# A state-space and butterfly block on one core: projection onto delta, B, C in two column halves, state products in two row halves of the array

## The chip, the cores and the metric

One Trainium2 chip, one of its cores. The metric is the device time of one execution in microseconds, the median over several. Engines: TensorE (PE), VectorE (DVE), ScalarE (ACT), GpSimd (POOL), SyncE (SP). All data is float32; three-part products in float32r are used in some places.

## The reference, cut to what matters

Input `x` is (2, 2048, 256). A state-space block and a feed-forward block are added to it one after the other, each on a layer norm.

```python
xz = einsum('bld,ed->ble', layernorm(x), in_proj_w); x_inner, z = split(xz, 2)
x_conv = silu(causal_conv4(x_inner) + conv_b)            # 512 channels
x_dbl = einsum('bld,ed->ble', x_conv, x_proj_w)          # 33 columns
delta = softplus(x_dbl[..., 0]); B = x_dbl[..., 1:17]; C = x_dbl[..., 17:]
# for every token: h = h * exp(delta * A) + x_conv * (delta * B);  y = sum_n h * C
y = (y + x_conv * D) * silu(z)
x = x + einsum('bld,od->blo', y, out_proj_w)
# feed-forward: expand to 1024, butterfly, gelu, butterfly, contract to 256
x = x + ffn(layernorm(x))
```

## The kernel before, in words

The sequence is cut into four tiles of 512 tokens; a loop runs over them, and each tile holds both batch rows (b0 and b1). The butterfly stages are multiplied into the weights in a preparation at the start, which runs beside tile 1. Every engine has its own instruction stream with an order written out by hand (`first_half`, `second_half`), and engines meet in semaphores. PE writes into three rings of PSUM banks: `wide` (3 banks, in-projection, x-projection, y, out-projection, up), `small` (3 banks) and `acc` (2 banks, down). `WIDE_ORDER` lists the uses of the wide ring in the order of PE (L60 to L66); use number n has bank n modulo 3 (L104), and `free` makes PE wait until all earlier takes of that bank are done.

In a tile, for one batch row: the in-projection (L727) gives x_inner and z; ACT copies and applies the first tap (L1060), DVE the three others (L1346), ACT the silu (L1069). `x_projection` (L731 to L737) multiplies the four channel blocks of xc with w_x, 33 columns, into rows 0 to 32 of one bank. ACT copies the result to xdT (L1077). `tokens_first` (L745) transposes xc in 16 pieces into four small banks, which ACT and DVE copy to x_tok (two each), and `xd_tokens_first` (L753) transposes xdT in four pieces; DVE copies 33 columns of each as xd (L1374) and goes on to softplus (L1377 to L1402), which yields delta, dB and the rest of the scan's inputs.

The scan is computed in matrices: m_mat (L1481, L1486) holds how tokens of a group of 128 act on each other, and `state` holds the state that enters each of the four groups, at rows 32c to 32c+15 for group c; c_startT has rows 32c to 32c+15 filled for the 128 tokens of group c alone. `state_inputs` (L795) makes four products of 16 weight columns each, at rows 32c of a bank. `advance_state` (L1454) makes the states. `ssm_output` (L820 to L837) then computes y: for channel blocks in pairs (0, 1), (2, 3), four products of x_tok with m_mat for each block (L829), then one product of state with c_startT over all 128 rows and 512 tokens for each block (L836). `gate` (L1488 to L1496) reads one y bank per block with xc and skip, and multiplies with z. After four gates the out-projection starts (L847), which waits for all of them.

The order on PE: b0's `x_projection`, `tokens_first`, `xd_tokens_first`, four in-projections of b1, the scan's small products mixed with three more in-projections, `x_projection` of b1, `ssm_output` of b0, `tokens_first` and `xd_tokens_first` of b1, out-projection of b0, small products of b1, in-projection 7 of b1, transposes for the feed-forward. Then the feed-forward of b0 (L858 up, L869 down), with `ssm_output` of b1 between up block 3 (with down block 1) and up block 4, and the out-projection of b1 after down block 2; then the feed-forward of b1. On DVE b0's gates are followed by the copies of x_tok and xd of b1, softplus of b1, the first residual (L1502) and the second normalisation (L1255).

## Time and profile before

| what | value |
|---|---|
| median of 3 runs | 631.44 us (630.95 to 631.99) |
| the profiled execution | 632.72 us, its span 630.8 us |
| PE busy | 560.5 us, 89% of the span |
| DVE busy | 443.5 us, 70% |
| ACT busy | 303.1 us, 48% |
| POOL busy | 123.9 us, 20% |
| mean granted clock of TensorE | 0.951 |
| DMA | 12.88 MB, mean 20 GB/s |

The span is that of the instructions of the program in the one execution that was profiled. Busy time is the union of an engine's instructions. A float32 product of PE leaves two records in the trace. The ends of PE's records are modelled, so consecutive records overlap a little; the distance between starts is the more exact figure. The granted clock is 1.00 at 2.4 GHz and 0.50 at 1.2 GHz.

### The profile page before, as it was taken

The page shows a single profiled execution, that of the slowest core. Times are in us where ns is not written, and L with a number is a line of the kernel's source. Part 1 is how long each engine was busy: PE and PEld are TensorE (multiplying, and loading weights), DVE is VectorE, ACT ScalarE, POOL GpSimd, SP SyncE. Part 2 cuts the span into 40 slices and gives each one's busy share as a digit, 9 for nine tenths or more (in the row PEclk, how much of TensorE's full clock was granted, in tenths as well). Part 3 has the DMA queues.
Part 4 walks back from the last instruction along what each step waited for, and adds up shares of the span by engine and source line. Part 5 has one row for each costly group of instructions (what it writes and reads, how often), then busy time and mean ns, then how long its engine had stood idle before and what let it go on. Part 6 is the DMA issues. An engine that isn't in the chain of part 4 may idle for free.

```text
span 630.8 us, 8980 instructions
## 1 busy us (share of the span) xinstructions
PE 560.5 (89%) x2996; PEld 436.9 (69%) x2996; DVE 443.5 (70%) x883; ACT 303.1 (48%) x511; POOL 123.9 (20%) x104
## 2 busy tenths in 40 slices
PE   4989776679999997979999989979999988979996
PEld 3747345647899773747899665847899664848895
DVE  5748868876556789877556699887555699977432
ACT  3655739146055766044144866054254865162252
POOL 4213100240012032250021042250020041340010
PEclk9988876899999999979999998979999999979999
DMA  8332020010010100010000000000100000000000
GB/s 239 4 22 4 0 66 2 1 35 2 3 64 2 34 1 2 0 34 0 33 33 0 33 0 0 0 33 0 33 33 0 33 0 0 0 0 2 0 34 34
DMA packets 33067, 12.88 MB, mean 20 GB/s; under 512 B 22003, under 2 KB 32499, under 8 KB 33044
## 3 DMA queue, kind: packets, MB, share of 16 engines
q1 hardware_dynamic: 31444, 9.96, 7.3%
q10 hardware_dynamic: 1600, 2.62, 1.2%
q8 instruction: 13, 0.21, 0.2%
q14 instruction: 10, 0.08, 0.0%
HBM read 8.39 MB, written 4.19 MB: 20 GB/s over the span
## 4 chain that ended last, share of the span: by engine, by line
PE 58%; DVE 23%; ACT 8%; issue 7%; DMA 2%; POOL 1%; DVEq 0%; ACTq 0%; POOLq 0%
PE acc L869 14%; PE wide L858 12%; PE wide L727 8%; DVE xc L1346 6%; PE wide L847 4%; PE wide L829 4%; PE wide L836 4%; PE wide L736 3%; DVE x1b_xn L1255 2%; PE small L717 2%; DVE soft L1385 2%; PE acc L656 1%; PE small L806 1%; DVE diag_sum L1475 1%; PE small L784 1%
## 5 line engine op out<-in xcount | busy, mean ns | idle before, releaser
L1031 ACT ACTIVATE hid_f<-wide,bias_up 128x512 f32<-128x512 f32 x64 | 44.0, 687 | 139.3 <-PE acc L869 127.4
L1346 DVE SCALAR_TENSOR_TENSOR xc<-xi,taps,xc 128x512 f32<-128x512 f32 x96 | 91.0, 958 | 6.5 <-ACT xc L1060 4.2
L1363 DVE TENSOR_TENSOR hid_low<-hid_f,hid_high 128x512 fp32r<-128x512 f32 x64 | 44.3, 692 | 68.8 <-ACT hid_high L1132 68.2
L869 PE MATMUL acc<-w_down_high,hid_high 128*128 128x256 f32 x256 | 73.9, 289 | 1.5 <-DVE hid_low L1363 1.5
L869 PE MATMUL acc<-w_down_low,hid_high 128*128 128x256 f32 x256 | 71.8, 281 | 0.0
L869 PE MATMUL acc<-w_down_high,hid_low 128*128 128x256 f32 x256 | 71.7, 280 | 0.0
L847 PE MATMUL wide<-w_out,yg 128*128 128x256 f32 x256 | 56.9, 380 | 0.0
L537 POOL TENSOR_TENSOR c_place<-xd,row_in_block 128x1024 f32<-128x1024 f32 x8 | 15.5, 1938 | 208.8 <-DVE xd L1374 208.8
L727 PE MATMUL wide<-xnT_high,w_in_high 128*128 128x512 f32 x128 | 54.9, 429 | 0.0
L858 PE MATMUL wide<-xnT_high,w_up_high 128*128 128x512 f32 x128 | 53.4, 417 | 0.0
L869 PEld LDWEIGHTS acc<-w_down_high,hid_high 128*128 128x128 f32 x256 | 48.2, 188 | 6.6 <-DVE hid_low L1363 4.5
L847 PEld LDWEIGHTS wide<-w_out,yg 128*128 128x128 f32 x256 | 48.0, 190 | 6.6
L727 PE MATMUL wide<-xnT_low,w_in_high 128*128 128x512 f32 x128 | 52.2, 408 | 0.0
L727 PE MATMUL wide<-xnT_high,w_in_low 128*128 128x512 f32 x128 | 52.0, 406 | 0.0
L858 PE MATMUL wide<-xnT_high,w_up_low 128*128 128x512 f32 x128 | 50.3, 393 | 0.0
L858 PE MATMUL wide<-xnT_low,w_up_high 128*128 128x512 f32 x128 | 50.1, 391 | 0.0
L869 PEld LDWEIGHTS acc<-w_down_low,hid_high 128*128 128x128 f32 x256 | 48.3, 189 | 1.8
L501 POOL TENSOR_TENSOR rstd<-var_eps,minus_half 128x4 f32<-128x4 f32 x16 | 19.0, 1186 | 154.5 <-DVE var_eps L1250 154.2
L869 PEld LDWEIGHTS acc<-w_down_high,hid_low 128*128 128x128 f32 x256 | 48.4, 189 | 0.0
L829 PEld LDWEIGHTS wide<-m_mat,x_tok 128*128 128x128 f32 x256 | 33.6, 209 | 18.2 <-ACT xdT L1031 10.3
L829 PE MATMUL wide<-m_mat,x_tok 128*128 128x128 f32 x256 | 35.1, 296 | 10.0 <-ACT xdT L1031 9.1
L1132 ACT ACTIVATE hid_high<-hid_f 128x512 fp32r<-128x512 f32 x64 | 40.6, 634 | 2.0
(184 smaller groups left out, 1136.4 us busy)
## 6 DMA issues: line engine op xcount, KB each, us to landing
x_in<-in_L_attn_x_dram SPq DMA_DIRECT2D x8, 512.0 KB, 3.6
out_dram<-x1b_xn SPq DMA_DIRECT2D x8, 512.0 KB, 2.9
xc<-in_L_attn_in_proj_w_dram ACTq DMA_DIRECT2D x2, 512.0 KB, 6.6
xc<-in_L_ffn_W_exp_dram ACTq DMA_DIRECT2D x1, 1024.0 KB, 9.3
low_w<-in_L_ffn_W_con_dram SPq DMA_DIRECT2D x1, 1024.0 KB, 5.6
raw_out<-n_L_attn_out_proj_w_dram ACTq DMA_DIRECT2D x1, 512.0 KB, 10.3
low_w<-in_L_ffn_up_weights_dram SPq DMA_DIRECT2D x14, 4.0 KB
low_w<-_L_ffn_down_weights_dram SPq DMA_DIRECT2D x14, 4.0 KB
```

The source lines that it names most:

```text
L501: pool.tensor_tensor(rstd[:, slot, :], var_eps[:, slot, :], minus_half[:, :], ALU.pow)\
L727: last = pe.matmul(bank[:, :], w_in[w][:, m, e * P:(e + 1) * P], xnT[x][:, m, :], start=n == 0, stop=n == MB * len(PASSES) - 1)
L736: last = pe.matmul(bank[0:XD, :], w_x[:, g, :], xc[b][:, g, :], start=g == 0, stop=g == CB - 1)
L829: pe.matmul(bank[:, c * P:(c + 1) * P], x_tok[:, c, g * P:(g + 1) * P], m_mat[:, c * P:(c + 1) * P], start=c == 0, stop=False, skip_group_ ...
L836: mark_written(pe.matmul(tile_of("y", g, b)[:, :], state[b][:, g * P:(g + 1) * P], c_startT[:, :], start=False, stop=True, skip_group_chec ...
L847: last = pe.matmul(bank[:, q * DM:(q + 1) * DM], yg[:, g, c * P:(c + 1) * P], w_out[:, g, :], start=g == 0, stop=g == CB - 1)
L858: last = pe.matmul(bank[:, :], w_up[w][:, m, j * P:(j + 1) * P], xnT[x][:, m, :], start=n == 0, stop=n == MB * len(PASSES) - 1)
L869: last = pe.matmul(acc[:, c, :], hid[h][:, j % HRING, c * P:(c + 1) * P], w_down[w][:, j, 0:DM], start=j == 0 and c % 2 == 0 and n == 0, s ...
L1031: ins = act.activation(out_ap, in_ap, how.pop("func"), **how)
L1132: act.activation(hid[0][:, j % HRING, :], hid_f32[:, j % HRING, :], ACT.Copy).then_inc(hid_high.handle, 1)
L1346: ins = dve.scalar_tensor_tensor(xc[b][:, e, :], xi[:, e, tap:tap + TILE], taps[:, e, tap:tap + 1], xc[b][:, e, :], ALU.mult, ALU.add)
L1363: dve.tensor_tensor(hid[1][:, j % HRING, :], hid_f32[:, j % HRING, :], hid[0][:, j % HRING, :].bitcast(F32), ALU.subtract).then_inc(hid_re ...
```

## The change

`x_projection`: w_x becomes 64 columns wide for each channel block (33 filled, the rest zero), blocks 0 and 2 write rows 0 to 63 of the bank, blocks 1 and 3 rows 64 to 127. ACT copies all 128 rows to xdT. Instead of four transposes of xdT with the identity there are four products of xdT with `fold`, a 128x33 matrix that adds rows j and 64+j. `ssm_output`: a y bank holds 256 tokens of two channel blocks instead of 512 tokens of one. The product of the states is cut into rows 0 to 63 (token half 0) and rows 64 to 127 (token half 1), each 256 columns wide and each writing its own bank; PE waits for both banks of a pair before the pair's first product. `gate` reads its block from the two neighbouring banks with one pattern, waits for both at the first block of a pair, and releases both after the first operation of the second block. The wide ring gets its banks from a list, so that the banks of a pair are neighbours. In the preparation w_x is cleared by POOL in place of xdT, `fold` is made by DVE ahead of its other constants and waited for by PE at preparation step 4, and bias_raw lies in yg.

```diff
-    + [("y", g, 0) for g in range(CB)] + [("out", 0, 0), ("out", 1, 0), ("in", 7, 1)]
-    + [("up", j, 0) for j in range(4)] + [("y", g, 1) for g in range(CB)]
+    + [("y", n, 0) for n in range(CB)] + [("out", 0, 0), ("out", 1, 0), ("in", 7, 1)]
+    + [("up", j, 0) for j in range(4)] + [("y", n, 1) for n in range(CB)]
...
+WIDE_BANKS = [2, 0, 1] * 5 + [2, 0] + [1, 2, 0, 1] + [2, 0, 1] + [2, 0, 1, 2] + [0, 1, 1, 2] + [0, 1, 2] * 4 + [0, 1]
...
-        w_x = sb("w_x", [P, CB, XD])
+        w_x = sb("w_x", [P, CB, HALF])
+        fold = sb("fold", [P, XD])
...
-        wide = [ctx.enter_context(nc.psum_tensor(f"wide{i}", [P, TILE], F32)) for i in range(RING)]
+        wide_banks = ctx.enter_context(nc.psum_tensor("wide", [P, RING, TILE], F32))
+        wide = [wide_banks[:, i, :] for i in range(RING)]
...
-        bias_raw = sb("bias_raw", [P, 2, DM])
+        bias_raw = yg[:, 0, :].rearrange("p (n d) -> p n d", d=DM)
...
-            pool.memset(xdT[:, :], 0.0).then_inc(zeroed, 1)
+            pool.memset(w_x[:, :, :], 0.0).then_inc(zeroed, 1)
...
                     wait_taken(pe, ("w_x", 0, 0))
+                    pe.wait_ge(folded, 1)
...
-                    last = pe.matmul(bank[0:XD, :], w_x[:, g, :], xc[b][:, g, :], start=g == 0, stop=g == CB - 1)
+                    at = HALF * (g % 2)
+                    last = pe.matmul(bank[at:at + HALF, :], w_x[:, g, :], xc[b][:, g, :], start=g < 2, stop=g >= CB - 2,
+                                     skip_group_check=True)
...
-                    last = pe.transpose(bank[:, c * P:(c + 1) * P], xdT[:, c * P:(c + 1) * P], ident[:, :])
+                    last = pe.matmul(bank[:, c * P:c * P + XD], xdT[:, c * P:(c + 1) * P], fold[:, :], start=True, stop=True)
...
-                for pair in ((0, 1), (2, 3)):
-                    for g in pair:
-                        bank = tile_of("y", g, b)
-                        free(pe, k, "y", g, b)
-                        if g == 0:
-                            read(pe, k, "moff", 0, b)
+                for pair in range(2):
+                    banks = [tile_of("y", 2 * pair + h, b) for h in range(2)]
+                    for h in range(2):
+                        free(pe, k, "y", 2 * pair + h, b)
+                    if pair == 0:
+                        read(pe, k, "moff", 0, b)
+                    for q in range(2):
+                        g = 2 * pair + q
                         for c in range(GR):
-                            pe.matmul(bank[:, c * P:(c + 1) * P], x_tok[:, c, g * P:(g + 1) * P],
-                                      m_mat[:, c * P:(c + 1) * P], start=c == 0, stop=False, skip_group_check=True)
-                    for g in pair:
-                        if g == 0:
-                            read(pe, k, "ct", 0, b)
-                            pe.wait_ge(first_state.handle, first_state.value(k, b, 1))
-                            pe.wait_ge(states_ready.handle, states_ready.value(k, b, 1))
-                        mark_written(pe.matmul(tile_of("y", g, b)[:, :], state[b][:, g * P:(g + 1) * P], c_startT[:, :],
-                                               start=False, stop=True, skip_group_check=True), "y", g, b)
+                            at = q * HALF_TILE + c % 2 * P
+                            pe.matmul(banks[c // 2][:, at:at + P], x_tok[:, c, g * P:(g + 1) * P],
+                                      m_mat[:, c * P:(c + 1) * P], start=q == 0 and c % 2 == 0, stop=False,
+                                      skip_group_check=True)
+                    if pair == 0:
+                        read(pe, k, "ct", 0, b)
+                        pe.wait_ge(first_state.handle, first_state.value(k, b, 1))
+                        pe.wait_ge(states_ready.handle, states_ready.value(k, b, 1))
+                    for q in range(2):
+                        g = 2 * pair + q
+                        for h in range(2):
+                            rows = slice(2 * SLOT * h, 2 * SLOT * (h + 1))
+                            last = pe.matmul(banks[h][:, q * HALF_TILE:(q + 1) * HALF_TILE],
+                                             state[b][rows, g * P:(g + 1) * P],
+                                             c_startT[rows, h * HALF_TILE:(h + 1) * HALF_TILE],
+                                             start=False, stop=q == 1, skip_group_check=True)
+                            if q == 1:
+                                mark_written(last, "y", 2 * pair + h, b)
...
-                take(k, "xp", 0, b, xdT[0:XD, :], tile_of("xp", 0, b)[0:XD, :])
+                take(k, "xp", 0, b, xdT[:, :], tile_of("xp", 0, b)[:, :])
...
+                dve.tensor_tensor(fold[:, :], ident[:, 0:XD], ident[:, HALF:HALF + XD], ALU.add).then_inc(folded, 1)
...
-                    dve.tensor_tensor(bias_out[:, :], bias_raw[:, 0, :], bias_raw[:, 1, :], ALU.add)
+                    link_setup(dve.tensor_tensor(bias_out[:, :], bias_raw[:, 0, :], bias_raw[:, 1, :], ALU.add))
...
-                written(dve, k, "y", g, b)
-                mark_read(dve.scalar_tensor_tensor(yg[:, g, :], xc[b][:, g, :], skip[:, g:g + 1],
-                                                   tile_of("y", g, b)[:, :], ALU.mult, ALU.add), "y", g, b)
-                read(dve, k, "y", g, b)
+                pair, q = divmod(g, 2)
+                bank = WIDE.bank(("y", 2 * pair, b))
+                both = wide_banks[:, bank:bank + 2, q * HALF_TILE:(q + 1) * HALF_TILE]
+                if q == 0:
+                    for h in range(2):
+                        written(dve, k, "y", 2 * pair + h, b)
+                halves = "p (h t) -> p h t"
+                ins = dve.scalar_tensor_tensor(yg[:, g, :].rearrange(halves, h=2),
+                                               xc[b][:, g, :].rearrange(halves, h=2), skip[:, g:g + 1],
+                                               both, ALU.mult, ALU.add)
+                if q == 0:
+                    link(ins)
+                else:
+                    mark_read(ins, "y", 2 * pair, b)
+                    read(dve, k, "y", 2 * pair, b)
+                    dve.sem_inc(WIDE.read[WIDE.bank(("y", 2 * pair + 1, b))], 1)
```

## Rows read from the trace of the kernel before

**Rows 1.** The page, part 4: the chain that ended last, shares by line.
```profile
PE acc L869 14%; PE wide L858 12%; PE wide L727 8%; DVE xc L1346 6%; PE wide L847 4%; PE wide L829 4%; PE wide L836 4%; PE wide L736 3%; DVE x1b_xn L1255 2%; PE small L717 2%; DVE soft L1385 2%; PE acc L656 1%; PE small L806 1%; DVE diag_sum L1475 1%; PE small L784 1%
```
**Rows 2.** Windows: length, busy us of PE, PEld, DVE, ACT, POOL, granted clock, DMA.
```profile
541.00:557.00 16.00, 11.79 (x64) 9.88 (x62) 15.10 (x42) 1.75 (x5) 10.31 (x7) 0.94 0.00 0
...
561.00:626.00 65.00, 64.26 (x388) 54.59 (x380) 31.31 (x52) 27.48 (x40) 5.32 (x3) 0.99 0.03 9
```
**Rows 3.** Timeline, PE, b0 of tile 4: start us, us, what, [idle before].
```profile
498.94 3.62 PE L736 MATMUL wide<-xc,w_x 128*33 128x512 f32 x8
...
504.39 0.65 PE L753 MATMUL small<-ident,xdT 128*128 128x128 f32 x4
```
**Rows 4.** Timeline, PE, around the output of b0, tile 4.
```profile
524.87 1.15 PE L816 MATMUL small<-c_hat,b_hat 128*128 128x128 f32 x8 [1.47 <-DVE diag L1470]
525.95 1.05 PE L795 MATMUL small<-x_tok,b_end 128*16 128x512 f32 x8
...
530.98 2.05 PE L829 MATMUL wide<-m_mat,x_tok 128*128 128x128 f32 x16 [0.43 <-DVE m_mat L1486]
533.40 1.96 PE L836 MATMUL wide<-c_startT,state 128*128 128x512 f32 x4 [0.37 <-DVE state L1454]
535.19 1.95 PE L829 MATMUL wide<-m_mat,x_tok 128*128 128x128 f32 x16
536.97 1.88 PE L836 MATMUL wide<-c_startT,state 128*128 128x512 f32 x4
```
**Rows 5.** Timeline, ACT, b0 of tile 4.
```profile
500.34 1.08 ACT L1031 ACTIVATE xnT_high<-small 128x512 fp32r<-128x512 f32 x2
502.66 0.59 ACT L1031 ACTIVATE xdT<-wide 33x512 f32<-33x512 f32 x1 [1.24 <-PE wide L736]
```
**Rows 6.** Timeline, DVE, b0 of tile 4.
```profile
505.27 0.28 DVE L1374 COPY xd<-small 128x132 f32<-128x132 f32 x1
...
534.63 0.75 DVE L1493 SCALAR_TENSOR_TENSOR yg<-xc,skip,wide 128x512 f32<-128x512 f32 x1 [0.59 <-PE wide L836]
...
536.02 0.74 DVE L1493 SCALAR_TENSOR_TENSOR yg<-xc,skip,wide 128x512 f32<-128x512 f32 x1
...
538.04 0.75 DVE L1493 SCALAR_TENSOR_TENSOR yg<-xc,skip,wide 128x512 f32<-128x512 f32 x1 [0.55 <-PE wide L836]
```
**Rows 7.** Timeline, PE, x-projection of b1 in tile 3.
```profile
388.69 3.59 PE L736 MATMUL wide<-xc,w_x 128*33 128x512 f32 x8 [1.35 <-ACT xc L1069]
392.22 2.05 PE L829 MATMUL wide<-m_mat,x_tok 128*128 128x128 f32 x16
```
**Rows 8.** Timeline, PE, preparation and tile 1.
```profile
74.09 5.11 PE L736 MATMUL wide<-xc,w_x 128*33 128x512 f32 x8 [2.51 <-ACT xc L1069]
...
100.52 3.78 PE L829 MATMUL wide<-m_mat,x_tok 128*128 128x128 f32 x16 [9.15 <-ACT xdT L1031]
```
**Rows 9.** Timeline, PE, the output of b1 in tile 4.
```profile
577.09 1.95 PE L829 MATMUL wide<-m_mat,x_tok 128*128 128x128 f32 x16
578.88 1.88 PE L836 MATMUL wide<-c_startT,state 128*128 128x512 f32 x4
...
583.41 0.81 PE L847 MATMUL wide<-w_out,yg 128*128 128x256 f32 x3
```
**Rows 10.** Timeline, DVE, the gates of b1 in tile 4.
```profile
577.92 0.74 DVE L1493 SCALAR_TENSOR_TENSOR yg<-xc,skip,wide 128x512 f32<-128x512 f32 x1
...
579.94 0.75 DVE L1493 SCALAR_TENSOR_TENSOR yg<-xc,skip,wide 128x512 f32<-128x512 f32 x1 [0.55 <-PE wide L836]
...
582.10 0.69 DVE L1496 TENSOR_TENSOR yg<-yg,z 128x512 f32<-128x512 f32 x1
```
**Rows 11.** Lines by form: xcount | busy us, mean ns | idle before.
```profile
L1529 DVE TENSOR_TENSOR x1b_xn<-acc,x1b_xn 128x1024 f32<-128x1024 f32 x8 | 9.8, 1225 | 6.3 <-PE acc L869 6.3
```
**Rows 12.** Windows with a stop of PE in tiles 4 and 3.
```profile
516.00:522.00 6.00, 2.99 (x14) 1.81 (x14) 5.93 (x8) 2.42 (x4) 4.23 (x3) 1.00 0.00 0
375.00:384.00 9.00, 6.00 (x16) 3.39 (x15) 8.89 (x11) 2.83 (x5) 5.19 (x3) 0.64 0.00 0
```

More of the change, by code:

```diff
@@ L53 @@
 SLOT = 32
+HALF_TILE = TILE // 2
+HALF = P // 2
 LOW = 7
@@ L78 @@
 HRING = 2
-FIRST_HALF_STEPS, VECTOR_STEPS = 45, 54
+FIRST_HALF_STEPS, VECTOR_STEPS = 47, 58
 class Signal:
@@ L94, with __init__ @@
 class Banks:
-    def __init__(self, nc, ctx, name, tiles, order):
+    def __init__(self, nc, ctx, name, tiles, order, banks=None):
         self.tiles, self.order = tiles, order
+        banks = banks or [n % len(tiles) for n in range(len(order))]
+        assert len(banks) == len(order)
         self.written = [ctx.enter_context(nc.semaphore(f"{name}{i}_written")) for i in range(len(tiles))]
@@ L102, in __init__ @@
         self.place, self.products, self.takes = {}, [0] * len(tiles), [0] * len(tiles)
-        for n, use in enumerate(order):
-            bank = n % len(tiles)
+        for use, bank in zip(order, banks):
             before = self.takes[bank]
@@ L217, in bass_preln_ssm_butterfly_ffn @@
         rstd = sb("rstd", [P, 2 * BATCH, GR])
-        wide = [ctx.enter_context(nc.psum_tensor(f"wide{i}", [P, TILE], F32)) for i in range(RING)]
+        wide_banks = ctx.enter_context(nc.psum_tensor("wide", [P, RING, TILE], F32))
+        wide = [wide_banks[:, i, :] for i in range(RING)]
         small = [ctx.enter_context(nc.psum_tensor(f"small{i}", [P, TILE], F32)) for i in range(RING)]
         acc = ctx.enter_context(nc.psum_tensor("acc", [P, GR, DM], F32))
-        WIDE = Banks(nc, ctx, "wide", wide, WIDE_ORDER)
+        WIDE = Banks(nc, ctx, "wide", wide, WIDE_ORDER, WIDE_BANKS)
         SMALL = Banks(nc, ctx, "small", small, SMALL_ORDER)
@@ L318, in bass_preln_ssm_butterfly_ffn @@
         rates_exp = sem("rates_exp")
+        folded = sem("folded")
         made = sem("made")
@@ L636, in make @@
                     for g in range(CB):
-                        last = pe.transpose(bank[:, g * XD:(g + 1) * XD], raw_x[:, g * P:(g + 1) * P], ident[0:XD, 0:XD])
+                        last = pe.transpose(bank[:, g * HALF:g * HALF + XD], raw_x[:, g * P:(g + 1) * P], ident[0:XD, 0:XD])
                 elif name == "w_out":
@@ L996, in receive @@
                 if name == "w_x":
-                    ins = act.activation(w_x[:, :, :].rearrange(flat), bank[:, 0:CB * XD], ACT.Copy)
+                    act.wait_ge(zeroed, 1)
+                    ins = act.activation(w_x[:, :, 0:XD], bank[:, 0:CB * HALF].rearrange("p (g w) -> p g w", w=HALF)[:, :, 0:XD],
+                                         ACT.Copy)
                 elif name == "w_out":
```

## The prediction

> **What bounds the kernel now.** I read the page's chain that ended last first: most of it lies on PE's lines, with L1346 of the vector engine among them, and the lines of the change hold 4% (L829), 4% (L836) and 3% (L736) of it [rows 1]. Then the timeline of one steady tile (the last, 484 to 626 us) by engine, since a share says nothing of which engine ends a stage. It shows stages with different limits. From the x-projection of batch 0 to the end of its second normalisation the vector engine sets the pace: between 541 and 557 us it is busy for 15.10 of 16.00 us and PE for 11.79 [rows 2]. From 561 us to the end PE is busy for 64.26 of 65.00 us [rows 2]: a microsecond won or lost on PE there is one of the whole. Between them lie hand-overs, which the other rows show. Four tiles run, each with a call of every function for batch 0 (b0) and batch 1 (b1); tile 1 overlaps the preparation of the weights and goes otherwise.
>
> **X-projection.** Now eight records (an fp32 product leaves two) of 512 columns in 3.62 us, in one column group [rows 3]. With neighbouring g in two column halves, two run at once. No row has two halves, but the state-input products (L795) write four column groups of 512 columns with the same operand size, and their eight records take 1.05 us, not 3.6 [rows 4]: one column group's own time. So two halves should take half, some 1.85 us: 1.75 us less per call (the end of the last record doesn't shrink); bounds are 0 (no overlap) and 1.8. Behind it the four transposes of xdT (0.65 us [rows 3]) become four fp32 products, eight records that each load 128 weight columns; the nearest row, eight fp32 records of 128 columns (L816), takes 1.15 us, the last of them 1.1 after the first began [rows 4]. I take +0.45 us, bounds 0 and +0.5.
> What reaches the end, b0, tiles 2 to 4: the first xp copy on ACT stands at 502.66 because it waited 1.24 us for L736; before it ACT finishes xnT_high at 500.34+1.08 = 501.42 [rows 5]. So the copy can come 1.24 us earlier, not 1.75, and x_tok, whose banks the later transposes need, goes with it. The transposes then end sooner by 1.24, and the products of xdT cost 0.45 more; part of this is hidden, since the vector engine's copy of x_tok stands between. The vector engine takes xd at 505.27 [rows 6]; I put it at 504.3, **1.0 us earlier**, and all of the vector stage follows. Three times: -3.0.
> b1, tiles 2 and 4: after L736 the first L829 waits 0.43 us, until 530.98, for m_mat of the vector engine [rows 4]. The 1.75 us become idle time of PE: **0**. In tile 3 L736 started late (388.69, after a wait for ACT's xc) and L829 follows it without a gap [rows 7]; there 1.3 us count, as the last activation limits it: -1.3. In the preparation (tile 1) b0's x-projection follows the activations one by one, and nothing comes of it; b1's, 5.11 us and partly at a lower clock [rows 8], stands ahead of products on which a load and the mixing wait. About 1.5 us there, less 0.45 for the xdT products of b0: -1.0.
>
> **State products.** Two (four records) of 512 columns take 1.88 us modelled and hold PE for 1.72, since 0.16 of a group lies beside its successor [rows 9, 4]. They become four products of 64 rows by 256 columns, eight records; if both row halves run at once, 0.86 us. Nothing in this trace uses row halves. Bounds: 0.86 (the column groups' behaviour, L795) and 1.72 (all eight in turn: 2048 product columns, as now). I take 0.86, as the only packed row of the trace overlaps fully. The Trainium skill's page "TensorE: Matmul & The Clock Gate" (Part 3, measured speedup) gives 3.07x for four row tiles, not 4x; an estimate by that efficiency is 1.12 us a pair, and 3.6 us more for the kernel. Changing the array's shape: L795 starts 0.07 us before its predecessor's modelled end, where products of one shape overlap by 0.16 to 0.17 [rows 4]; so 0.1 us per change, two in the path of each call: 0.2 us. The skill's "TensorEngine Tiling (Array Packing)" (Key Properties) says that a mode change drains the engine; by this rule, the trace agrees, at 0.1 us.
>
> **The wait that this needs.** The y banks now hold token halves of two channel blocks, so gate 0 needs the whole first pair, and a bank is free only when gate 1 has read it. WIDE_BANKS gives the second pair of b0 banks 0 and 1, of which 1 is the first pair's; that of b1 banks 1 and 2, 1 again. PE asks for both banks before any product of the second pair. Now y2 needs neither, and y3 only gate 0. So PE stops after the first pair until gate 1's first operation ends, with all 16 x_tok products, the state products, and then the transposes of b1 (or up block 4 and down block 2) queued behind it; gates 2 and 3 wait for the same.
> b0, tiles 2 and 4: state products start at 533.40, gate 0 at 534.63, when y0 is done [rows 4, 6]; with 0.86 us for the whole pair that stays. Gate 1's first operation ends at 536.02+0.74 = 536.76 [rows 6]. Then 1.78 us of L829 (start to start [rows 4]) and 0.86 of L836, and the 0.37 us from the end of the stream to a gate (533.40+0.86 to 534.63): gate 2 at about 539.8, against 538.04 now [rows 6]. **+1.8**, with shape changes +2.0. Its cover would be slack behind the gates, and there is none: x_tok, xd and softplus follow at once, and the vector engine has 0.9 us idle in the next 16 [rows 2]. Tile 3 runs the same once its x-projection is shorter. Three times: +6.0. Tile 1's second pair waits 9.15 us for ACT's xdT [rows 8], long after gate 1: 0.
> b1, all tiles, PE-bound: L829 of the second pair at 577.09, its L836 at 578.88 [rows 9]. After: gate 1's first operation ends at 577.92+0.74 = 578.66 [rows 10], 0.1 to hand on, 1.78+0.86: PE is through at 581.4, against 578.88+1.72 = 580.6. Gates 2 and 3 start at 581.8 and take 2.85 us (579.94 to 582.10+0.69 = 582.79 [rows 10]) to 584.65. Up block 4 and down block 2 (2.8 us, from 580.6 to 583.41) fill PE till 584.2, so the out-projection waits for the gates: 584.75 against 583.41 [rows 9], **+1.35**, with shape changes +1.5. Four times: +6.0.
>
> **Small edits.** The gate reads two banks through one pattern: the final add, 1024 columns over two banks, takes 1225 ns [rows 11], 0.61 us per 512, so no surcharge; bounds 0 and 0.1 a gate. The copy of xdT takes 128 rows for 33, the same 512 columns as its neighbours (1.08 us for two, 0.59 for xdT [rows 5]): 0. `fold` is one add of 33 columns, less than the 0.28 us of a 132-column copy [rows 6], in the preparation ahead of the x-projection: covered by the wait for activations there, 0.2 if not. The memset of w_x takes the place of xdT's and is smaller; bias_raw within yg and its link add one wait of under 0.1.
>
> **Sum.** -3.0 -1.3 -1.0 +6.0 +6.0 = +6.7 us on the profiled execution's 632.72, which is 1.28 above the median of 631.44. Against the median: **638.0 us**.
>
> **Rivals.** (1) The row halves don't overlap: +0.86 a pair, 1.72 a call, seven calls: +12, 650 us. For it: no row shows row halves; against: L795. (2) The clock falls in the new gap. PE stops for about 2.5 us between the pairs, and in b0 already idles 2 us shortly before. Two stretches, in each of which PE stands still for 3 us, show a granted clock of 1.00 (from 516) and 0.64 (from 375), a mean over the levels 2.4 and 1.2 GHz [rows 12]: it can go either way. At half clock the second pair costs 2.6 us more; in three to four of seven calls: 646 us. (3) The other side, faster: the stop between the pairs is not there, or is filled, since the first pair is read sooner than I say. Its place is the wait for y's banks; it decides from the point where gate 1's read ends before the first pair's successor could start. Then b1 wins 1.72 a call (-6.9), b0 0.86 three times (-2.6), and the x-projection's 5.3 stand: -15, 617 us. Half of that if the stop is shorter only. Against it: gate 1 needs gate 0's two operations before it, 2.1 us after the pair. (4) Gains and stops even out: if the x-projection gives its full 1.75 in b0 and the stops cost 1 each, the sum is within 1 us of zero.
>
> **Chances.** Forecast 0.55, (1) 0.10, (2) 0.14, (3) 0.10, (4) 0.11. A measurement can tell about 0.2%, 1.3 us, from no change. Faster 0.12 (all of 3, a little of 4), same 0.08, slower 0.80. The range of the forecast alone is 634 to 642 (clock and bounds); taking in most of (2), part of (1) and the slow end of (4): 632 to 648.
>
> **What would show it.** Right: L736's eight records in about 1.9 us; L836's eight in about 1.0; PE idle some 2.5 us before every second L829 group of tiles 2 to 4, ended by the vector engine's yg; xd about 1 us earlier after the x-projection; the out-projection of b1 waiting for the gates. Wrong: no idle time before the second L829 group, L836 pairs at 1.8 us, or half clock behind the gap.

## The result, and the profile after

| | before | after |
|---|---|---|
| median | 631.20 us (630.52 to 631.99, 4 runs) | 648.68 us (644.92 to 650.34, 4 runs) |
| ratio, 95% interval | | 1.0264 (1.0237 to 1.0290) |
| profiled execution, its span | 632.72, 630.8 us | 649.47, 647.7 us |
| mean granted clock of TensorE | 0.951 | 0.941 |

Slower, as forecast, but by 17.5 us at the medians (16.9 at the spans) and not by 6.8: 0.7 us above the range. After's lines are numbered anew: L745 is the x-projection (before L736), L763 xdT by `fold` (L753), L842 x_tok by m_mat (L829), L853 the state products (L836), L868 the out-projection (L847), L1523 and L1532 the gate (L1493, L1496).

The page of after, parts 1 and 4, beside [rows 1]:
```profile
PE 555.4 (86%) x3092; PEld 446.1 (69%) x3092; DVE 443.8 (69%) x884; ACT 302.3 (47%) x511; POOL 122.7 (19%) x104
...
PE acc L890 13%; PE wide L879 9%; DVE xc L1370 7%; PE wide L735 5%; PE wide L842 5%; PE wide L868 4%; DVE yg L1523 3%; PE wide L853 3%; DVE x1b_xn L1278 2%; DVE diag_sum L1499 2%; PE small L725 2%; PE small L755 2%; DVE yg L1532 2%; PE acc L663 2%; DVE soft L1409 2%
```
PE is busy for 5 us less than before (560.5) in a span 17 us longer. The gate (L1523, L1532) is new in this list: 5% of the chain, some 30 us. Groups of instructions by line and form:
```profile
L1523 DVE SCALAR_TENSOR_TENSOR yg<-xc,skip,wide 128x512 f32<-128x512 f32 x32 | 23.8, 744 | 29.2 <-PE wide L853 29.1
L1532 DVE TENSOR_TENSOR yg<-yg,z 128x512 f32<-128x512 f32 x32 | 22.1, 692 | 3.0 <-DVE yg L1523 2.3
L853 PE MATMUL wide<-c_startT,state 64*128 64x256 f32 x128 | 19.5, 425 | 1.1 <-DVE state L1478 1.1
L745 PE MATMUL wide<-xc,w_x 128*64 128x512 f32 x64 | 19.2, 611 | 8.3 <-ACT xc L1092 8.3
```
The gate's read costs no more through two banks (744 ns; 743 before), but DVE waits 29.1 us for L853 ahead of it. The view of the one line L842 says what PE waited for ahead of it (us, times):
```profile
  ACT xdT L1054: 9.9, 1
  DVEq L1531: 9.8, 4
  DVE yg L1523: 6.8, 3
```
The first is tile 1's, as before [rows 8]. The other seven are new: a stop of 2.3 to 2.4 us before the second pair in every call but that one, released by gate 1's read (DVEq L1531 is the release of the second bank that stands behind it). Timeline, PE, the output of b0 in tiles 3 and 4 (start us, us, what, [idle before]), beside [rows 4, 7]:
```profile
399.33 2.05 PE L842 MATMUL wide<-m_mat,x_tok 128*128 128x128 f32 x16 [0.42 <-DVE m_mat L1510]
401.75 1.14 PE L853 MATMUL wide<-c_startT,state 64*128 64x256 f32 x8 [0.37 <-DVE state L1478]
405.17 2.05 PE L842 MATMUL wide<-m_mat,x_tok 128*128 128x128 f32 x16 [2.28 <-DVE yg L1523]
407.15 1.14 PE L853 MATMUL wide<-c_startT,state 64*128 64x256 f32 x8
408.21 2.00 PE L755 MATMUL small<-ident,xc 128*128 128x128 f32 x16
...
541.97 2.05 PE L842 MATMUL wide<-m_mat,x_tok 128*128 128x128 f32 x16
544.39 1.14 PE L853 MATMUL wide<-c_startT,state 64*128 64x256 f32 x8 [0.37 <-DVE state L1478]
547.80 3.49 PE L842 MATMUL wide<-m_mat,x_tok 128*128 128x128 f32 x16 [2.28 <-DVE yg L1523]
551.22 1.13 PE L853 MATMUL wide<-c_startT,state 64*128 64x256 f32 x8
555.60 1.75 PE L868 MATMUL wide<-w_out,yg 128*128 128x256 f32 x7 [0.40 <-DVE yg L1532]
```
The same instructions behind the same stop take 2.05 us in tile 3 and 3.49 in tile 4. The windows over tiles 4 and 3 (second and third line) show why; the first line is one of the preparation (length, busy us of PE, PEld, DVE, ACT, POOL, granted clock):
```profile
128.00:140.00 12.00, 8.38 (x32) 5.65 (x30) 8.17 (x17) 3.82 (x8) 6.40 (x4) 0.73 0.15 46
546.00:552.00 6.00, 4.20 (x24) 3.99 (x24) 2.40 (x4) 0.00 (x0) 0.00 (x0) 0.72 0.00 0
403.00:409.00 6.00, 3.83 (x31) 3.34 (x32) 3.37 (x5) 0.09 (x1) 0.00 (x0) 1.00 0.00 0
```
The granted clock is a mean of 1.2 and 2.4 GHz in the first two lines, and 2.4 GHz throughout in the third. Of the seven second pairs three ran for the most part at half clock (at 161, 261 and 548 us). On DVE the stop looks like this (timeline, gates of b0 in tile 4), beside [rows 6]:
```profile
545.61 0.75 DVE L1523 SCALAR_TENSOR_TENSOR yg<-xc,skip,wide 128x512 f32<-128x512 f32 x1 [0.59 <-PE wide L853]
...
547.00 0.74 DVE L1523 SCALAR_TENSOR_TENSOR yg<-xc,skip,wide 128x512 f32<-128x512 f32 x1
547.90 0.69 DVE L1532 TENSOR_TENSOR yg<-yg,z 128x512 f32<-128x512 f32 x1 [0.16 <-DVE yg L1523]
552.48 0.75 DVE L1523 SCALAR_TENSOR_TENSOR yg<-xc,skip,wide 128x512 f32<-128x512 f32 x1 [3.88 <-PE wide L853]
...
555.37 1.28 DVE L1393 COPY x_tok<-small 128x512 f32<-128x512 f32 x2
```
And b1 of tile 4 on PE at full clock, beside [rows 9]:
```profile
588.13 1.95 PE L842 MATMUL wide<-m_mat,x_tok 128*128 128x128 f32 x16
590.01 1.13 PE L853 MATMUL wide<-c_startT,state 64*128 64x256 f32 x8
593.59 2.05 PE L842 MATMUL wide<-m_mat,x_tok 128*128 128x128 f32 x16 [2.44 <-DVEq L1531]
595.57 1.13 PE L853 MATMUL wide<-c_startT,state 64*128 64x256 f32 x8
...
599.98 1.32 PE L868 MATMUL wide<-w_out,yg 128*128 128x256 f32 x5 [0.22 <-DVE yg L1532]
```

**Where the time came from.** How late each stage of after begins against the same stage of before, from the starts of L842, L868 and L745, gives the terms of the 16.9 us:

| term | forecast | measured |
|---|---|---|
| x-projection, L745 of b0 to the first L842 of b0, tiles 2, 3, 4 | -1.0, -2.3, -1.0 | -0.85, -2.9, -0.9 |
| output of b0, first L842 to L868, tiles 2, 3, 4 | +2.0 each | +3.6, +2.7, +3.6 |
| output of b1, first L842 to L868, tiles 1 to 4 | +1.5 each | +3.5, +1.9, +1.9, +2.0 |
| preparation and tile 1 up to b1's output | -1.0 | +1.65 |
| everything between | 0 | +0.7 |
| sum | +6.7 | +16.9 |

The three calls with a half-clock second pair are the +3.6, +3.6 and +3.5; without the clock a call of b0 costs +2.1 and one of b1 +1.9 to +2.0. Tile 3 needs care: there before's first pair had no wait for m_mat and state (9.46 us from L829 to L847, in tiles 2 and 4 10.06), so 0.6 us of its +2.7 is a wait that has moved, and its -2.9 holds a half clock of before (before_warm below).

### The profile page after: what moved, and what is told of

The parts are those of the page before. It is cut to its first block, busy times and chain, and to the rows that moved or that the text cites. A ratio compares the mean times of both kernels' runs of the same rounds, so it can differ in the third digit from the quotient of the medians.

```text
span 647.7 us, 9206 instructions
## 1 busy us (share of the span) xinstructions
PE 555.4 (86%) x3092; PEld 446.1 (69%) x3092; DVE 443.8 (69%) x884; ACT 302.3 (47%) x511; POOL 122.7 (19%) x104
## 4 chain that ended last, share of the span: by engine, by line
PE 47%; DVE 32%; ACT 10%; issue 8%; DMA 2%; POOL 1%; DVEq 1%; ACTq 0%; POOLq 0%
PE acc L890 13%; PE wide L879 9%; DVE xc L1370 7%; PE wide L735 5%; PE wide L842 5%; PE wide L868 4%; DVE yg L1523 3%; PE wide L853 3%; DVE x1b_xn L1278 2%; DVE diag_sum L1499 2%; PE small L725 2%; PE small L755 2%; DVE yg L1532 2%; PE acc L663 2%; DVE soft L1409 2%
## 5 line engine op out<-in xcount | busy, mean ns | idle before, releaser
L842 PE MATMUL wide<-m_mat,x_tok 128*128 128x128 f32 x256 | 40.0, 321 | 27.2 <-ACT xdT L1054 9.9
L842 PEld LDWEIGHTS wide<-m_mat,x_tok 128*128 128x128 f32 x256 | 37.1, 230 | 34.9 <-ACT xdT L1054 10.7
L868 PE MATMUL wide<-w_out,yg 128*128 128x256 f32 x256 | 57.2, 382 | 2.2 <-DVE yg L1532 1.8
L868 PEld LDWEIGHTS wide<-w_out,yg 128*128 128x128 f32 x256 | 48.0, 190 | 9.5 <-issue 2.3
L508 POOL TENSOR_TENSOR rstd<-var_eps,minus_half 128x4 f32<-128x4 f32 x16 | 17.3, 1084 | 164.2 <-DVE var_eps L1273 163.9
L1523 DVE SCALAR_TENSOR_TENSOR yg<-xc,skip,wide 128x512 f32<-128x512 f32 x32 | 23.8, 744 | 29.2 <-PE wide L853 29.1
```

Of the source, the lines that this page charges most:

```text
L508: pool.tensor_tensor(rstd[:, slot, :], var_eps[:, slot, :], minus_half[:, :], ALU.pow)\
L842: pe.matmul(banks[c // 2][:, at:at + P], x_tok[:, c, g * P:(g + 1) * P], m_mat[:, c * P:(c + 1) * P], start=q == 0 and c % 2 == 0, stop=False,
L868: last = pe.matmul(bank[:, q * DM:(q + 1) * DM], yg[:, g, c * P:(c + 1) * P], w_out[:, g, :], start=g == 0, stop=g == CB - 1)
L1523: ins = dve.scalar_tensor_tensor(yg[:, g, :].rearrange(halves, h=2), xc[b][:, g, :].rearrange(halves, h=2), skip[:, g:g + 1], both, ALU.mu ...
```

## Experiments

Each was run beside the kernel before, on the same chip; a ratio is to that. The sets ran on different chips, so what an experiment gives back against after (17.5 us over its own before) is told as the difference of the two distances to before. The theory: the time goes to the stop between the pairs, as forecast, and the excess over 6.7 us to the clock behind the stops. The rivals: row halves that don't overlap; a gain of the x-projection that isn't there; longer gate and hand-over chains.

### The halves of the change

**x_only** has the projection half alone: w_x 64 columns wide, the products with `fold`, the preparation's edits; `ssm_output`, `gate` and the order of the banks are those of before.

> Only the projection half of the change (two column halves, all 128 rows copied, products with fold in place of the transposes); ssm_output, the gates and the banks are those of before. Theory A (the stop between the pairs of y and what it does to the clock are the whole loss): faster than before by 3 to 6 us, 625 to 628, xd about 1 us earlier after the x-projection of b0, b1's saving lost in the wait for m_mat. Rival B (the x-projection gives less than its share, and is part of why the change cost more than forecast): 631 or more.

629.86 us (627.31 to 635.0), ratio 0.9973 (0.9953 to 0.9993): faster, but between the two cases (625 to 628, 631 or more). **states_only** has the other half alone, with `x_projection` of before.

> Only the other half: row halves, pairs of banks, one pattern over two banks in the gate. Theory A: as slow as the whole change plus what the projection gave, 651 to 655. Rival B: no slower than the whole change, 646 to 649.

653.25 us (647.68 to 656.35), ratio 1.0334 (1.0286 to 1.0383). The loss is all in the state half; the projection half is faster than before, by 1.45 us at the medians (0.4 to 3.0 by the interval), about a quarter of the 5.3 us that I had summed for it. The timeline of x_only on PE, tile 4:
```profile
525.25 2.54 PE L745 MATMUL wide<-xc,w_x 128*64 128x512 f32 x8 [1.31 <-ACT xc L1081]
527.93 2.05 PE L839 MATMUL wide<-m_mat,x_tok 128*128 128x128 f32 x16
...
537.43 1.08 PE L763 MATMUL small<-fold,xdT 128*128 128x33 f32 x8
538.34 7.15 PE L857 MATMUL wide<-w_out,yg 128*128 128x256 f32 x32
```
b1's projection waits for ACT's xc, so its saving turns into idle time. The products with `fold` of b1 stand on PE right ahead of the out-projection and hold it for 0.91 us from start to start, where the transposes took 0.57 (540.47 to 541.04 in the timeline of before): 0.34 us that I had counted for b0 alone.

### Do the row halves overlap?

**full_rows**: the whole change, but each state product over all 128 rows (c_startT is zero in the rows that this adds).
```diff
-                                             state[b][rows, g * P:(g + 1) * P],
-                                             c_startT[rows, h * HALF_TILE:(h + 1) * HALF_TILE],
+                                             state[b][:, g * P:(g + 1) * P],
+                                             c_startT[:, h * HALF_TILE:(h + 1) * HALF_TILE],
```


> The whole change, but the products of the states run over all 128 rows, 256 tokens each, in the same banks and with the same waits (the other half's rows are zero for these tokens). Theory A (row halves overlap and save 0.75 to 0.86 us a pair, on the path of every call but the first): 10 to 12 us slower than the changed kernel, 658 to 661. Rival C (row halves win nothing, since loading their weights or the change of shape costs as much): within 2 us of the changed kernel, 647 to 651.

658.70 us (658.17 to 660.17), ratio 1.0435 (1.0413 to 1.0457). Timeline, PE, tile 4:
```profile
553.98 2.05 PE L842 MATMUL wide<-m_mat,x_tok 128*128 128x128 f32 x16 [2.22 <-DVE yg L1522]
555.87 1.89 PE L852 MATMUL wide<-c_startT,state 128*128 128x256 f32 x8
557.60 1.95 PE L755 MATMUL small<-ident,xc 128*128 128x128 f32 x16
```
Eight records hold PE for 1.73 us here (555.87 to 557.60) and for 1.06 in after (407.15 to 408.21). They overlap, and are worth 10 us: without them the change costs 27. The clock doesn't make this difference: full_rows too has three of its seven second pairs at half clock (at 306, 453 and 600 us).

### Is it the stop?

**stop_alone**: the kernel before, in which PE waits for gate 1's read ahead of the second pair, and nothing else.
```diff
                         free(pe, k, "y", g, b)
+                        if g == 2:
+                            read(pe, k, "y", 1, b)
```


> The kernel before with one wait more: PE waits for gate 1's read before the second pair of y. Nothing else of the change. Theory A: 1.7 us in each of seven calls, 643, and up to 5 us more from stretches at half clock, 643 to 648; PE idle about 1.7 us before every second group of x_tok products. Rival D (the stop is hidden by slack behind the gates, the loss is elsewhere in the new layout): 631 to 634.

642.40 us (641.36 to 643.38), ratio 1.0175 (1.0154 to 1.0195): +11.1 us for one wait. The view of its line L831, what PE waited for ahead of it (us, times):
```profile
  DVE yg L1495: 10.1, 7
```
Seven stops of 1.4 us (I expected 1.7), since the state products of before keep PE busy longer behind the first pair. None of the seven second pairs ran at half clock. In the profile a call of b1 costs 1.6 to 1.8 us more and one of b0 1.1; the stretches ahead of b0's output, with half clock behind c_start in all three tiles, add 1.1 in all. Rival D is excluded: one shared wait costs 11 us even where the layout is the old one. It isn't the price in the new layout, where the stop is longer and the row halves give part of it back: there the seven calls cost 14.7 us at full clock (19.2 less 4.5 of half clock), and the forecast had 12.

### Is the excess the clock's?

**stops_warm**: after, with eight products of the identity with itself, into a small bank that is free, in each stop of the loop.
```diff
+            def keep_warm(out_ap, n):
+                for _ in range(n):
+                    pe.matmul(out_ap, ident[:, :], ident[:, :], start=True, stop=True)
...
                 for pair in range(2):
+                    if pair and (b or not isinstance(k, int)):
+                        use = ("ln2T", 0, 1) if b else ("xtok", 0, 1)
+                        free(pe, k, *use)
+                        keep_warm(tile_of(*use)[:, 0:P], 8)
```


> The whole change, and in the stop between the pairs of y eight fp32 products of the identity (1.8 us of the 2.3 us) into a small bank that is free then; nothing waits for them. Theory A (part of the loss is real work at half clock, because PE stood still just before): the stretches at half clock behind the stops go, those at the wait for c_start and after the second normalisation stay, 4 to 6 us less than the changed kernel, 642 to 645. Rival E (half clock comes where it comes, whatever stands in the stop): no difference, 647 to 650, or slower if the products delay the second pair.

644.56 us (643.83 to 645.21), ratio 1.0219 (1.0193 to 1.0245). Timeline, PE, tile 4, and the window of the second pair:
```profile
541.34 2.05 PE L719 MATMUL small<-ident 128*128 128x128 f32 x16
543.69 2.05 PE L850 MATMUL wide<-m_mat,x_tok 128*128 128x128 f32 x16 [0.29 <-DVE yg L1531]
```
```profile
546.00:552.00 6.00, 5.60 (x41) 4.83 (x38) 4.58 (x9) 1.29 (x3) 0.53 (x1) 1.00 0.00 0
```
The second pair takes 2.05 us again, and the clock is 2.4 GHz. Through before, 3.4 us are back, with work whose result nobody uses; the intervals of the two ratios still overlap a little, so the size is better read from the traces. From the first x_tok products to the out-projection the three calls that stood at +3.5, +3.6 and +3.6 are at +1.9, +2.1 and +2.1 in stops_warm, 4.5 us less, and the other four haven't moved by 0.05 us. Nothing but PE's idling was changed.

**prep_warm** adds to stops_warm that the product of the preparation ahead of a stop of 5.3 us is made six times (`for q in list(range(4)) * (6 if (i, h) == (0, 1) else 1)`).

> stops_warm (644.6, ratio 1.0219) with one further edit: in the preparation the product that stands ahead of a stop of 5.3 us (116 to 121.5) is made six times over, so that PE works through most of the stop. In the changed kernel PE works at half clock from 120.5 to 134.5 and its products at 130.3 take 3.78 us, in the kernel before 1.99, and from there the changed kernel is 1.7 to 1.9 us late. If that lateness is the clock's: 642.5 to 643.3. If it is the engines' order, or the lost time is covered elsewhere in the preparation, as the half clock behind the waits for c_start was: 644 to 645.

645.38 us (642.68 to 649.73), ratio 1.0241 (1.0204 to 1.0277): inconclusive, and in neither of its two cases. The runs spread over 7 us. In the profile of stops_warm b1's first output begins 0.3 us after that of before and not 1.65, though nothing was changed in the preparation; in those of gate_order, fill_both and gates_warm, with the same preparation, 0.4 us sooner to 0.1 later, in full_rows 0.6 later, in gates_fill 5.0. So the +1.65 belongs to the profiled execution of after, a median has probably less of it, and how much stays open.

**before_warm**: is half clock always a cost? The kernel before has it too, behind the wait for c_start and at the second normalisation; identity products were put ahead of those waits.
```diff
+                        if m == 0 and (name, b) == ("ln2T", 0) and not isinstance(k, int):
+                            keep_warm(bank[:, c * P:(c + 1) * P], 4)
...
                 free(pe, k, name, 0, b)
+                if (name, b) == ("ct", 0) and not isinstance(k, int):
+                    keep_warm(bank[:, 0:P], 10)
```


> The kernel before, with ten products of the identity while PE waits for c_start of b0, and four ahead of each wait for a normalised block of b0's feed-forward (tiles 2 to 4). Nothing else. It measures what half clock after a wait costs the old kernel: 20 us of PE work ran at half clock in these stretches of its profile, so up to 10 us, of which the part after the normalisation (7 us) lies on the chain. Theory A: 623 to 627. Rival E: no gain, 631 or slower by what the products delay.

631.30 us (629.24 to 632.78), ratio 1.0003 (0.9988 to 1.0018). The windows of [rows 12], in it:
```profile
516.00:522.00 6.00, 5.32 (x35) 4.08 (x34) 5.93 (x8) 2.46 (x5) 4.23 (x3) 1.00 0.00 0
375.00:384.00 9.00, 7.87 (x45) 5.79 (x43) 8.82 (x12) 4.65 (x9) 5.80 (x3) 1.00 0.00 0
```
The clock of the second went from 0.64 to 1.00, its mean over the run from 0.951 to 0.970, and the time stayed; my expectation of 623 to 627 was wrong. Stage by stage the half clock was not all free. Timeline, PE, x-projection of b1 in tile 3, beside [rows 7]:
```profile
387.16 3.19 PE L742 MATMUL wide<-xc,w_x 128*33 128x512 f32 x7
...
391.20 2.05 PE L837 MATMUL wide<-m_mat,x_tok 128*128 128x128 f32 x16 [0.42 <-DVE m_mat L1494]
```
The x-projection, L742 here (seven of its eight records are in the line), doesn't start late any more. From L736 of b0 to this L829 tile 3 takes 34.11 us in before and 32.04 here, as tiles 2 and 4 do in both; 0.60 of these 2.07 us go again by the out-projection, in waits for DVE, so the half clock behind c_start had cost tile 3 some 1.5 us. Behind the second normalisation it had cost nothing: from the out-projection of b0 to b1's output before takes 32.53 to 32.55 us, and this kernel, at full clock, 0.25 us more, as the added products stand in the way; in after it takes 32.53 to 32.56 us in all three tiles, though the half clock in it lasts twice as long in tile 3 as in tiles 2 and 4. DVE sets the pace there ([rows 2], 15.10 of 16.00 us). With 0.7 us more in the preparation, where nothing was changed, the profiled execution gains nothing in sum, nor does the median.

**x_c_warm** puts the same products ahead of the c_start wait of x_only.

> Only the half of the change in the projection, with ten identity products ahead of PE's wait for the decays of c_start, and nowhere else. x_only read 629.9 where the counted savings gave 625 to 628, and it worked at half clock behind that wait in all three tiles, the kernel before in one. If the clock took the missing 2 to 3 us: 626 to 628. If the saving was lost to the other engines instead (the projection ends earlier, but its reader and the norms of the next half do not), it stays within 0.2% of x_only: 629 to 630.5.

629.34 us (626.43 to 631.7), ratio 0.9957 (0.9937 to 0.9978), not to be told from x_only's 0.9973. The window 516 to 522 us of x_only, then of x_c_warm:
```profile
516.00:522.00 6.00, 5.84 (x19) 3.50 (x20) 5.93 (x9) 1.20 (x2) 3.44 (x2) 0.72 0.00 0
```
```profile
516.00:522.00 6.00, 4.32 (x19) 2.71 (x20) 5.93 (x9) 2.80 (x5) 3.45 (x2) 1.00 0.00 0
```
In tile 2, where the half clock of x_only lasted longest, the products win 1.0 us from L745 to the first x_tok products (32.20 to 31.20), and 0.6 of it is gone by the out-projection. The clock is not what keeps x_only from its 5 us.

### Can the stop be filled or shortened?

**gate_order**: after, but DVE does both reads of a pair first, then both multiplies, so the banks come free one multiply earlier.
```diff
+                if g % 2:
+                    return
...
+                both = [dve.scalar_tensor_tensor(yg[:, g + q, :].rearrange(halves, h=2),
+                                                 xc[b][:, g + q, :].rearrange(halves, h=2), skip[:, g + q:g + q + 1],
+                                                 wide_banks[:, bank:bank + 2, q * HALF_TILE:(q + 1) * HALF_TILE],
+                                                 ALU.mult, ALU.add) for q in range(2)]
+                mark_read(both[1], "y", g, b)
+                read(dve, k, "y", g, b)
+                dve.sem_inc(WIDE.read[WIDE.bank(("y", g + 1, b))], 1)
+                for q in range(2):
+                    dve.tensor_tensor(yg[:, g + q, :], yg[:, g + q, :], z[b][:, g + q, :], ALU.mult)\
+                        .then_inc(gated.handle, 1)
```


> The whole change, but the vector engine reads both blocks of a pair first and multiplies both with z after that, so the banks are released one multiplication (0.7 us) sooner. Theory A: 0.7 us less in each of seven calls, 5 us in all, 642 to 645. Rival D (the stop is not what ends the stage): 647 to 650.

641.17 us (639.87 to 642.54), ratio 1.0163 (1.0135 to 1.0192): 6.8 us back. In the profile the stops are 0.73 us shorter (1.55 in b0, 1.71 in b1), a call 0.85, and still three of seven second pairs ran at half clock (at 158, 257 and 585 us). **fill_both**: after, with three of the four blocks of transposes of b1 between the pairs of b0, down block 2 between those of b1, and down block 3 ahead of the out-projection.
```diff
-                ssm_output(k, 0)
-                tokens_first(k, 1)
+                ssm_output(k, 0, lambda: tokens_first(k, 1, range(3)))
+                tokens_first(k, 1, range(3, GR))
...
-                ssm_output(k, 1)
-                ffn(k, 0, 4, 5)
+                ssm_output(k, 1, lambda: down(k, 0, 2))
+                up(k, 0, 4)
+                down(k, 0, 3)
...
-                ffn(k, 0, 5, HB)
+                up(k, 0, 5)
+                ffn(k, 0, 6, HB)
```


> The whole change, with real work moved into the stop: three of the four transposed blocks of b1 in b0's call, down block 2 in b1's call, and down block 3 ahead of the out-projection. Theory A: b1 wins down block 2's 1.4 us in each of four calls, b0 only what the clock gives back (about 1.6 us where it fell), 640 to 643. Rival D: 647 to 650.

641.98 us (641.2 to 644.03), ratio 1.0192 (1.0164 to 1.0219): 6.0 us back. No second pair ran at half clock in its profile, but the out-projection of b0 did in two of the three tiles of the loop (8.83 us where it takes 7.15):
```profile
547.21 8.83 PE L870 MATMUL wide<-w_out,yg 128*128 128x256 f32 x32 [0.88 <-DVE yg L1536]
```
So the half clock has in part moved and not gone. **gates_fill** has both edits.

> The whole change with both repairs together: DVE does the two scalar_tensor_tensors of a pair first and then its two multiplies (alone 641.2), and PE has other work in the stop (three transposed blocks in b0, a down product in b1; alone 642.0). Theory A, the stop is PE's idle time between the pairs of banks, and the two repairs work on the same idle time (one shortens it, the other fills it): the gains of 7.5 and 6.7 us don't add up, 637 to 640, and the rest over the old kernel (630.5 to 631.3) is what no repair touches, the hand-over of the last gates and the preparation. Theory B, they work on different terms (stop on one side, number of DVE hand-overs on the other): 634 to 636.

633.92 us (631.94 to 640.35), ratio 1.0029 (1.0012 to 1.0046): 15.4 us back, so the gains at least add up (6.8 + 6.0 = 12.8), and theory A is excluded. The profiles show the different terms of theory B: the order makes each call 0.85 us shorter, and the filling takes 1.4 us out of the stretch behind each call of b1, since PE has done that work already. The profiled execution was the slowest of the eleven, but its order is plain; PE and then DVE, b0 of tile 3:
```profile
398.10 1.13 PE L855 MATMUL wide<-c_startT,state 64*128 64x256 f32 x8 [0.36 <-DVE state L1482]
399.17 1.53 PE L755 MATMUL small<-ident,xc 128*128 128x128 f32 x12
400.79 2.05 PE L844 MATMUL wide<-m_mat,x_tok 128*128 128x128 f32 x16
...
399.33 1.41 DVE L1526 SCALAR_TENSOR_TENSOR yg<-xc,skip,wide 128x512 f32<-128x512 f32 x2 [0.58 <-PE wide L855]
```
Both reads are over 1.41 us after gate 0 begins, the transposes fill the time till then, and L844 starts with no wait. **gates_warm** has the order of gate_order with the products of stops_warm.

> The whole change with the gates in the other order and eight identity products in each stop of the loop, which only keep PE's clock. gate_order alone read 641.2 with more half clock work than the changed kernel (63.7 against 61.0 us of busy PE), stops_warm alone gained 4.1. If that half clock work is what gate_order still pays for: 637 to 638. If the shorter stop of gate_order leaves no time for the eight products before the bank is free (0.7 us shorter), they delay the second pair and it stays at 640 to 642.

639.19 us (638.31 to 640.21), ratio 1.0112 (1.0089 to 1.0134), between its two cases: keeping the clock is worth 3.3 us on top of the order, doing real work in the stop 8.6. The calls of the profiles side by side, from the first x_tok products to the out-projection, against before (tile 3 of b0 without its moved 0.6 us, half clock without its 1.4 to 1.6 us):

| | stop in b0, b1 | call of b0 | call of b1 | second pairs at half clock |
|---|---|---|---|---|
| after | 2.28, 2.44 | +2.1 | +1.9 to 2.0 | 3 of 7 |
| stops_warm | filled | +2.1 | +1.9 to 2.0 | none |
| stop_alone | 1.46, 1.36 to 1.56 | +1.1 | +1.6 to 1.8 | none |
| gate_order | 1.55, 1.71 | +1.3 | +1.0 to 1.2 | 3 of 7 |
| gates_warm | filled | +1.4 | +1.0 to 1.2 | none |

Not tried: asking for the two banks one by one. Only bank 1 is shared by the two pairs, so the products of the second pair that write its other bank could start before gate 1's read, with no other work moved. The whole change, even so repaired, is 0.3% behind the kernel before, and x_only remains the one part that beats both kernels; x_c_warm adds nothing that can be told.

## Why the prediction was wrong in size

**Right, by its steps.** The mechanism and the sign: PE asks for both banks, gate 1's read releases them, and the second pair, b1's transposes and gates 2 and 3 stand behind it. Forecast was a stop of 2.5 us, measured 2.28 to 2.44. The out-projection of b1 waits for the gates. L745 takes 1.94 us in b0 (forecast 1.85), the row halves overlap, a gate's read pays nothing for two banks. For b0 at full clock the working was good to 0.1 us: gate 0 to the copy of x_tok is 8.31 us in tile 3 (402.98 to 411.29) against 6.18 before (534.63 to 540.81), so +2.1 where the forecast had +2.0. That the time lies near the 650 us of rival (1) is no support for it: full_rows excludes it.

**What the forecast missed** is 10.2 of the 16.9 us of the profiled execution: 4.5 half clock behind the stops, 2.65 the preparation, 1.7 the calls of b1 and 1.0 those of b0 besides the clock (0.6 of it the wait that moved in tile 3), 0.7 between the stages, less 0.35 that the x-projection gave more.

**The step that failed: the clock was a rival with a chance, and should have been a term of the sum.** Rival (2) said "at half clock the second pair costs 2.6 us more; in three to four of seven calls: 646 us", at 0.14. It happened in three of seven, at 1.4 to 1.5 us each in b0 (3.49 against 2.05), 1.6 in b1 of tile 1 (L842 3.23, L853 1.54): 4.5 us, by the table and by the same calls of stops_warm. Its price of 2.6 was too high, since the clock came back before the pair's end. The forecast let the two levels of [rows 12] stand as an open question and then summed at 2.4 GHz only; three or four stops at half clock belonged into the sum. The Trainium skill, "TensorE: Matmul & The Clock Gate", section "A second HAM failure mode: psum-queue depth-cycling", tells of another kernel whose PE idles briefly between groups of products, while it goes round its banks, and swings between both levels. By this rule, the trace agrees, in three of seven stops.

**Mis-sized: the calls of b1**, +1.9 at full clock in tiles 1 to 3 and +2.0 in tile 4, instead of +1.5. In tile 4, against the working of the forecast: gate 1's read ends 5.35 us after the first L842 (588.13 to 593.48), where I took the 5.07 of before (573.59 to 578.66), since gate 0 now waits for the whole pair; the second L842 takes 1.98 us to its L853 (593.59 to 595.57) and not 1.78; gates 2 and 3 take 2.98 us and not 2.85, as the last multiply waits 0.16 us for the read ahead of it, which now also releases a second bank; the hand-overs 0.08 more. That is 0.69 us, of which the forecast had 0.15 for changes of the array's shape. Half of the 0.20 at L842 stands in stop_alone too, 1.89 (541.88 to 543.77), where no shape changes.

**Mis-sized: the row halves.** I took 0.86 us for a pair; from start to start it is 1.06. By the Trainium skill's "TensorE: Matmul & The Clock Gate" (Part 3, measured speedup) the estimate was 1.12; by this rule, the trace agrees better than with my full overlap, though a shape change is within the 1.06.

**The x-projection** came out within the whole change (-4.65 for -4.3), in part by luck. The -1.3 for tile 3 was read from an L736 that starts late [rows 7], and it is late by the half clock of [rows 12]: before_warm, with the projection of before, has -2.07 in the same place. At equal clock the projection gives 0.85 us from L745 of b0 to the first L842 (forecast 1.0; in tile 4 of x_only xd comes 5.47 us after L745 begins, before 6.33). In x_only 0.34 of it goes again on b1's `fold` products ahead of the out-projection, which in after is hidden, where the gates end later anyway (the 0.40 us wait at 555.60). So a tile keeps 0.5 us, tile 1 gave 0.2 and not 1.0, and these make 1.7 us where the medians have 1.45. The profiled execution of x_only, 2.7 us shorter in its span, gained 0.3 us in tile 2, 1.7 in tile 3 and 0.5 in tile 4: tile 3 has the half clock of before in it, tile 2 lost some 0.4 to its own. How often before has that half clock in its other executions isn't known.

**The preparation**, +1.65 for -1.0, goes with half clock at 128 to 134 us in this execution (L686 took 3.78 us, before 1.99); states_only has both as well, half clock till 134 us and +1.56. As prep_warm settled nothing, the cause is argued, not shown. The -1.0 itself was too much: of six other profiles with this preparation none is 1.0 us early, and four lie within 0.4 us of before.

## What to carry to other kernels

Packing small products into row or column tiles saves what it says, but look first at what the new layout does to the ring of banks: here 0.67 us saved per pair cost a stop of 2.3 us, since both banks of a pair wait for both readers. Put a stop that comes from a shared bank at its full length into the sum, with half clock behind a part of them, and plan what PE does in it together with the change; reads of a bank come before any other work on its reader. Before you save from a stretch of the old trace, look at its granted clock: a stage that is late by half clock can win time without your change. Half clock counts only where PE's work is waited for: 1.5 us behind each stop here, 1.5 once behind c_start, nothing behind the normalisation.

## What the runs showed of the hardware

Stops of PE of only 2.3 to 2.4 us, between stretches of nearly full activity, were followed by half clock in three of seven places and not in four, the same instructions each time (after); stops of 1.55 to 1.71 us in three of seven too (gate_order), stops of 1.4 us in none (stop_alone). Behind three idle times of 0.8 to 0.9 us within 7 us half clock came in the out-projection, in two of the loop's three tiles (fill_both). Row halves with fp32 products of 256 columns: 1.06 us a group against 1.73 over all rows, a factor of 1.63. Column halves of 512 columns: 1.94 us against 3.62, 1.87. And restoring the clock from 0.951 to 0.970 on the mean left the time of the old kernel where it was.
